# A graph network on one core: layer 1's softmax per eight graphs, reloaded one-hots, and the sum over edges as one pass over high and low halves

## The reference

```python
g_l = (h @ W_l.T).reshape(b, n, H, F)          # H = 8 heads, F = 16
g_r = (h @ W_r.T).reshape(b, n, H, F)
g_sum = g_r[:, :, None, :, :] + g_l[:, None, :, :, :]
e = jnp.einsum('bijhf,f->bijh', jax.nn.leaky_relu(g_sum, SLOPE), w_attn)
mask = adj_mat[..., None]
e = e * mask
e = jnp.where(mask == 0, -jnp.inf, e)
a = jax.nn.softmax(e, axis=2)
attn_res = jnp.einsum('bijh,bjhf->bihf', a, g_r)
out = jax.nn.leaky_relu(attn_res.reshape(b, n, H * F), SLOPE)
```

## Time and profile before

| | |
|---|---|
| median of 3 runs | 1712.24 us (1710.98 to 1717.81) |
| the profiled execution | 1710.04 us |
| its span, first to last instruction | 1708.3 us |
| busy: TensorE, its weight loads, VectorE, ScalarE | 1495.2, 1280.6, 1247.5, 977.0 us |
| mean granted TensorE clock, of full speed | 0.953 |

### The profile page before, as it was taken

The page is one execution under the profiler, slowest core; times in us unless marked ns, Lnnn a source line. Parts: engine busy times, 40 slices in busy tenths (PEclk is TensorE's granted clock), DMA queues, the critical chain, the costliest instruction groups (busy, mean ns, idle before and its releaser), DMA issues. The chain is left out here.

```text
span 1708.3 us, 32251 instructions
## 1 busy us (share of the span) xinstructions
PE 1495.2 (88%) x9961; PEld 1280.6 (75%) x9961; DVE 1247.5 (73%) x2330; ACT 977.0 (57%) x2551; POOL 4.9 (0%) x24
## 2 busy tenths in 40 slices
PE   3664889999999999999999985999999999998655
PEld 2553567778777787777788774999999999997554
DVE  4886667877878777878778853566666666666788
ACT  2564755665556565566656522666666666665554
POOL 0000000000000000000000000000000000000000
PEclk9897889999999999999999998999999999999787
DMA  3220534334433443343334303867667667671122
GB/s 81 63 62 14 213 144 182 153 144 158 175 143 143 161 173 143 143 186 148 143 150 178 145 32 131 314 238 255 247 239 255 243 244 252 241 256 38 56 74 68
DMA packets 100673, 274.61 MB, mean 161 GB/s; under 512 B 8800, under 2 KB 51424, under 8 KB 100576
## 3 DMA queue, kind: packets, MB, share of 16 engines
q1 hardware_dynamic: 100176, 273.52, 43.8%
q10 hardware_dynamic: 400, 0.00, 0.0%
HBM read 143.46 MB, written 130.02 MB: 160 GB/s over the span
## 5 line engine op out<-in xcount | busy, mean ns | idle before, releaser
L827 DVE TENSOR_TENSOR b_vv<-bank,b_vv 128x512 f32<-128x512 f32 (+1 forms) x192 | 113.7, 599 | 156.5 <-ACT b_vv L753 153.1
L1130 DVE TENSOR_REDUCE c_var<-c_ysq 128x4 f32<-128x512 f32 (+1 forms) x192 | 114.0, 594 | 117.0 <-ACT c_ysq L1078 94.4
L722 PE MATMUL bank<-b_wt,b_SIT 128*128 128x136 f32 x1280 | 161.4, 281 | 29.6 <-DVE b_SJ L452 23.2
L657 PE MATMUL wide<-b_vv,put_w 128*128 128x512 f32 (+1 forms) x384 | 171.5, 528 | 11.3 <-DVE b_vv L827 9.4
L722 PEld LDWEIGHTS bank<-b_wt,b_SIT 128*128 128x128 f32 x1280 | 152.8, 190 | 36.9 <-DVE b_SJ L452 23.4
L1020 PE MATMUL wide<-W2c,c_h 128*128 128x128 f32 x1280 | 174.0, 275 | 0.0
L1020 PEld LDWEIGHTS wide<-W2c,c_h 128*128 128x128 f32 x1280 | 169.6, 193 | 4.3
L686 PE MATMUL bank<-b_grs,b_SJ 128*128 128x128 f32 x1280 | 163.9, 286 | 4.2 <-ACT b_os L802 4.2
L686 PEld LDWEIGHTS bank<-b_grs,b_SJ 128*128 128x128 f32 x1280 | 159.6, 201 | 9.3 <-issue 5.1
L1050 PEld LDWEIGHTS bank<-c_z,c_SIT 128*128 128x128 f32 x1280 | 154.4, 194 | 5.5 <-DVE c_z L1138 2.3
L1050 PE MATMUL bank<-c_z,c_SIT 128*128 128x128 f32 x1280 | 155.0, 277 | 2.1 <-DVE c_z L1138 2.1
(11 more groups left out here) (212 smaller groups left out, 3154.9 us busy)
## 6 DMA issues: line engine op xcount, KB each, us to landing
si_d<-b_SI SPq DMA_DIRECT2D x64, 640.0 KB, 3.0
sj_d<-b_SJ SPq DMA_DIRECT2D x64, 640.0 KB, 4.0
sit_d<-b_SIT SPq DMA_DIRECT2D x64, 640.0 KB, 4.9
c_SJ<-sj_d SPq DMA_DIRECT2D x64, 640.0 KB, 4.1
c_SI<-si_d SPq DMA_DIRECT2D x64, 640.0 KB, 5.2
c_SIT<-sit_d SPq DMA_DIRECT2D x64, 640.0 KB, 4.3
xin<-in_x_dram SPq DMA_DIRECT2D x16, 256.0 KB, 3.0
ain<-in_adj_dram SPq DMA_DIRECT2D x16, 256.0 KB, 3.3
```

The lines of the kernel that those rows point to most:

```text
L657: pe.matmul(out, e.put_w[:, pos % Q, :], vv[:, (pos + k) % 2, 0:width(k)], start=(pos % Q == 0), stop=False)
L722: d = pe.matmul(ring[0][:, 0:W], s.SIT[:, ms, j, :], wt[:, (pos - LAG) % 2, j, :], start=(j == 0), stop=(j == TILES - 1))
L827: v.tensor_tensor(vv[:, b, 0:w], bU[b][:, 0:w], vv[:, b, 0:w], ALU.max).then_inc(v_ok, 1)
L1130: v.tensor_reduce(var[:, k, 0:r], ysq[:, k, 0:width(k)].rearrange("p (j f) -> p j f", f=P), AX.X, ALU.add).then_inc(sum_ok, 1)
```

## The change

- Softmax goes by R = 8 graphs: `score` puts eight graphs into 64 + 64 rows, and the scans run on 64 rows instead of 32, in halves of 640 edges, at positions 0, 1 and 2 of eight. The exponentials' transposes are ten, in transpose mode, at position 3, into two banks.
- The lag of the gather back is 11 steps, and the sum comes one step later. SJ keeps 4 buffers and SIT 2 instead of 8. Both, and g_r, are read back from HBM (SJl, SITl, grl), issued by SyncE's queue thirteen graphs later.
- `wt` is split: ScalarE copies it to F32R (`wh`, its first 136 columns: the high halves), VectorE subtracts (`wl_ok`: the low halves in the next 136). The sum is one F32R pass of 272 columns per tile. ScalarE copies both halves of the result (`ol`, `os`), and the finish adds them.
- The first 16 steps are written out instead of 8 (`every_step` gets `first`, 2 here), and `put_w` and `put_m` are made for 8 graphs instead of 4 in the setup.

```diff
@@ -522,22 +475,69 @@
         def sem(name):
             return c.enter_context(nc.semaphore("b_" + name))
 
-        LAG = 6
+        LAG = 11
+        R = 8
         W = P + HEADS
...
@@ -608,22 +605,33 @@
...
+                                     s.SIT[:, b, :, :]).then_inc(sit_out[b], 16)
+                    m, b, r = n - 13, (pos - 13) % 2, 16 * (4 * K + (pos - 13) // 2 + 1)
+                    if inner or 0 <= m < B:
+                        if inner or m >= 2:
+                            sp.wait_ge(o_mm, n - 14)
+                        sp.wait_ge(sj_out[b], r)
+                        sp.wait_ge(gr_out[b], r)
+                        sp.wait_ge(sit_out[b], r)
+                        sp.dma_start(SJl[:, b, :], e.sj_v[:, m, :]).then_inc(sj_in[b], 16)
+                        sp.dma_start(grl[:, b, :], e.gr_v[:, m, :]).then_inc(gr_in[b], 16)
+                        sp.dma_start(SITl[:, b, :, :].bitcast(F32), e.sit_v[:, m, :].rearrange("p (j i) -> p j i", i=P)).then_inc(sit_in[b], 16)
+
+                every_step(sp, step, 13, 2)
                 for b in range(2):
...
@@ -633,18 +641,18 @@
 
             @block.tensor
             def _(pe):
-                def transpose_exponentials(half):
-
-                    for j in range(TILES // 2 * half, TILES // 2 * (half + 1)):
-                        o = pe.matmul(ring[2][:, H * j:H * j + H], top[:, P * j:P * j + P], e.ident[0:H, 0:H],
-                                      start=True, stop=True)
-                    return o
+                def transpose_exponentials(bank, half):
+                    for j in range(TILES // 2):
+                        a = P * (TILES // 2 * half + j)
+                        o = pe.transpose(bank[:, H * j:H * j + H], top[:, a:a + P], e.ident[0:H, 0:H])
+                    o.then_inc(at_mm, 1)
 
                 def step(K, pos, inner):
...
@@ -654,41 +662,53 @@
                     def score(k):
                         pe.wait_ge(v_ok, 3 * n + k + 1)
                         out = bE[:, chunk(k)]
-                        pe.matmul(out, e.put_w[:, pos % Q, :], vv[:, (pos + k) % 2, 0:width(k)], start=(pos % Q == 0), stop=False)
-                        pe.matmul(out, e.put_m[:, pos % Q, :], s.SI[:, pos % 4, chunk(k)], start=False,
-                                  stop=(pos % Q == Q - 1)).then_inc(e_mm, 1)
+                        pe.matmul(out, e.put_w[:, pos, :], vv[:, (pos + k) % 2, 0:width(k)], start=(pos == 0), stop=False)
+                        pe.matmul(out, e.put_m[:, pos, :], s.SI[:, pos % 4, chunk(k)], start=False,
+                                  stop=(pos == R - 1)).then_inc(e_mm, 1)
 
                     if A:
...
-                            pe.wait_ge(s.sit_ok, 3 * n + 2)
+                            pe.wait_ge(s.sit_ok, 3 * n + 3)
                         if inner or m > 0:
                             pe.wait_ge(w_ok, 3 * m)
-                        transpose_exponentials(0)
                     if A:
                         gather(1)
-                    if transposed(n, pos, inner):
-                        transpose_exponentials(1).then_inc(at_mm, 1)
-                    if inner or 0 <= n < B:
+                    if T:
+                        transpose_exponentials(ring[2], 0)
+                        transpose_exponentials(ring[0], 1)
+                    if O:
+                        pe.wait_ge(wl_ok, 3 * o + 3)
+                        pe.wait_ge(sit_in[ob], 16 * (4 * K + (pos - LAG - 1) // 2 + 1))
+                        if A:
+                            pe.wait_ge(s.sit_ok, 3 * n + 1)
+                        for j in range(TILES):
+                            d = pe.matmul(ring[1][:, 0:2 * W], SITl[:, ob, j, :], wh[:, ob, j, :],
+                                          start=(j == 0), stop=(j == TILES - 1))
+                        d.then_inc(o_mm, 1)
+                    if A:
                         pe.wait_ge(s.sit_ok, 3 * n + 3)
                     if S:
+                        pe.wait_ge(sj_in[mb], 16 * (4 * K + (pos - LAG) // 2 + 1))
+                        pe.wait_ge(gr_in[mb], 16 * (4 * K + (pos - LAG) // 2 + 1))
                         if inner or m > 0:
                             pe.wait_ge(w_ok, 3 * m)
-                            pe.wait_ge(os_ok, m)
                         for k in range(CHUNKS):
-                            if k == 2 and transposed(n, pos, inner):
-                                pe.wait_ge(at_ok, batches(K, pos))
+                            if k == 0 and T:
+                                pe.wait_ge(at_ok, 2 * K)
+                            if k == 1 and O:
+                                pe.wait_ge(os_ok, o + 1)
                             for j in tiles(k):
                                 d = pe.matmul(ring[k][:, P * (j - 4 * k):P * (j - 4 * k) + P],
-                                              s.SJ[:, ms, P * j:P * j + P].bitcast(F32), grs[:, ms, :], start=True, stop=True)
+                                              SJl[:, mb, P * j:P * j + P], grl[:, mb, :], start=True, stop=True)
                             d.then_inc(g_mm, 1)
...
@@ -713,26 +733,15 @@
                         pe.matmul(pair_bank(pos, 1)[:, 0:2 * P], s.xT[:, :], e.WlrT[:, :, :], start=True, stop=True).then_inc(s.p_mm, 1)
                     if A:
                         score(2)
-                    if S:
-                        pe.wait_ge(w_ok, 3 * m + 3)
-                        pe.wait_ge(wa_ok, m + 1)
-                        if N:
-                            pe.wait_ge(s.sj_ok, 3 * g + 1)
-                        for j in range(TILES):
-                            d = pe.matmul(ring[0][:, 0:W], s.SIT[:, ms, j, :], wt[:, (pos - LAG) % 2, j, :],
-                                          start=(j == 0), stop=(j == TILES - 1))
-                        d.then_inc(o_mm, 1)
                     if N:
                         pe.wait_ge(s.sib_ok, g + 1)
                         pe.wait_ge(s.sj_ok, 3 * g + 2)
                         transpose_rows(pe, e, s, ring[1], 0)
...
@@ -752,26 +761,39 @@
                             act.wait_ge(e_mm, 3 * n + k - 1)
...
+                            act.wait_ge(w_ok, 24 * K - 24)
+                            act.wait_ge(wa_ok, 8 * K - 8)
+                        act.copy(aT[:, TILES // 2 * half:TILES // 2 * (half + 1), :],
+                                 bank[:, 0:TILES // 2 * H].rearrange("p (j c) -> p j c", c=H)).then_inc(at_ok, 1)
+
                     if A:
                         slope(0)
-                    if transposed(n, pos, inner):
-                        act.wait_ge(at_mm, i)
...
-                        if inner or n > Q:
-                            act.wait_ge(z_ok, i - 1)
-                        act.copy(es[:, :], bE[0:2 * H, 0:ECAP]).then_inc(es_ok, 1)
+                        if inner or n > R:
+                            act.wait_ge(z_ok, K - 1)
+                        act.copy(es[:, :], bE[:, 0:ECAP]).then_inc(es_ok, 1)
+                    if O:
+                        act.wait_ge(o_mm, o + 1)
+                        if pos % Q == 0 and (inner or o >= 2 * Q):
+                            act.wait_ge(s.cen_ok, fours(K, pos))
+                        act.copy(ol[:, (pos // Q + 1) % 2, pos % Q, :], ring[1][:, W:2 * W])
+                        act.copy(os[:, (pos // Q + 1) % 2, pos % Q, :], ring[1][:, 0:W]).then_inc(os_ok, 1)
                     if S:
-                        q = (pos - LAG) % Q
-                        act.wait_ge(at_ok, softmaxes(K, pos))
+                        r = (pos - LAG) % R
+                        act.wait_ge(at_ok, 2 * eights(K, pos))
...
-                        act.wait_ge(o_mm, m + 1)
-                        if (pos - LAG) % Q == 0 and (inner or m >= 2 * Q):
-                            act.wait_ge(s.cen_ok, i - 2)
-                        act.copy(os[:, parity(pos), (pos - LAG) % Q, :], ring[0][:, 0:W]).then_inc(os_ok, 1)
+                        for k in range(CHUNKS):
+                            js = slice(tiles(k).start, tiles(k).stop)
+                            act.wait_ge(w_ok, 3 * m + k + 1)
+                            act.wait_ge(wa_ok, m + 1)
+                            if inner or m >= 2:
+                                act.wait_ge(o_mm, m - 1)
+                            act.copy(wh[:, mb, js, 0:W], wt[:, mb, js, :]).then_inc(wh_ok, 1)
                     if N:
-                        if inner or g >= 8:
-                            act.wait_ge(o_mm, g - 7)
-                            act.wait_ge(sit_out[(pos + 1) % 2], 16 * (4 * K + (pos + 1) // 2 - 3))
...
@@ -816,39 +840,47 @@
...
                         w, b = width(k), (pos + k) % 2
                         v.tensor_tensor(vv[:, b, 0:w], bU[b][:, 0:w], vv[:, b, 0:w], ALU.max).then_inc(v_ok, 1)
 
-                    z = Steps(v, seq_z, 3 * (i - 1))
-                    if softened(n, pos, inner):
-                        z.n = 3
+                    z = Steps(v, seq_z, 5 * (K - 1))
+
```

(60 more changed lines are left out.)

257 lines of the change are left out of this document (138 added, 119 removed).

## The result

| | before | after |
|---|---|---|
| median | 1711.61 us (1710.22 to 1717.81, 4 runs) | 1746.82 us (1744.98 to 1747.83, 4 runs) |
| span of the profiled execution | 1708.3 us | 1745.9 us |
| mean granted TensorE clock | 0.953 | 0.921 |
| busy: TensorE, weight loads, VectorE, ScalarE | 1495.2, 1280.6, 1247.5, 977.0 | 1436.9, 1209.4, 1303.8, 1051.5 |

The changed kernel is slower: ratio 1.0187, 95% interval 1.0164 to 1.0211. That is inside the forecast's range (1688 to 1755) and on the side it held likeliest, but 29 us above the 1718 that it named, and outside its own case's 1704 to 1732. TensorE has 58 us less work, as the change intends, and the kernel takes 38 us more.

A forecast was written before the change was run, and what follows sets the result against it. It took each step as bounded by the longer of TensorE and VectorE, VectorE in most positions. Last split 61 us earlier, drain +67 and setup +1.5 gave +7.5 us, so 1718; range 1688 to 1755.

The forecast's parts named there:

- the side it held likeliest: Whole kernel: slower, chance 0.48, against 0.27 for within 0.5% of 1712 us and 0.25 for faster.
- its own case: Whole kernel: the forecast's main account without the rivals, 1704 to 1732 us, chance 0.50.
- TensorE's sum: Plain step of layer 1: ten F32R matmuls of 272 columns take 1.2 us instead of 2.32, making the step 10.4.
- VectorE's list: Layer-1 loop: VectorE needs 8.7 us every step plus finishes, residuals and softmax parts; it sets positions 0, 1, 2, 4, 5.
- a sign of being wrong: Layer-1 loop: the forecast called itself wrong if steps 6 and 7 took over 11.5 us.
- in a plain step they end some 2 us after the split: Plain loop step: row copies queued behind waiting high copies end before TensorE's gather back needs them, costing nothing.
- 10.4 + 1.1 + 0.8: Position 3 of eight: TensorE's plain step, ten exponential transposes, and copying out both halves, 12.3 us.
- The clock in the loop: Layer-1 loop: 4 us of occasional low clock as before, plus 7 us after the pauses of positions 0 and 1.
- a rival of 0.15: Positions 0 and 1: pauses bring 1.2 GHz work, losing 4 to 5 us per eight, +30, 1750 us; chance 0.15.
- The drain: End of layer 1: 118 us plus 15 for half clock, 133 in place of 66, +67 us.
- The transfers: DMA traffic grows from 2.0 to 3.5 MB per graph, 8.5 us of a step of 10.8 or more, costed at nothing.
- the start: Layer 1's steps 0 to 10, up to the split of graph 11: forecast to end at 280.5 us.

The follow-up runs named there:

- three edits: Changed kernel with exponentials' transposes one place later, the drain's chain ahead of maxima and finishes, and TensorE kept busy in positions 0 and 1: 1687.51 us, ratio 0.983.
- the busy gaps alone: Changed kernel with 36 small unread bf16 matmuls filling TensorE's pause in positions 0 and 1 of every eight: 1732.48 us, ratio 1.009.
- the run with another order: Changed kernel with the drain's high copies and low subtractions directly behind the multiplication, ahead of finish, residual, squares and maxima: 1720.29 us, ratio 1.0041.

## Why the prediction was right and wrong

**TensorE's sum: right.** 1.2 us were taken by the F32R row of 512 columns; the changed kernel's sum takes 1.25 at full clock (952.54 to the next gather at 953.79).

**VectorE's list: right in its items, 1.3 us per eight short in the sum.** Low subtractions 1.70 (1.63 forecast), half scans 1.47 to 1.53. With the clock full and the wait of position 3 away, the splits are:

| position | 0 | 1 | 2 | 3 | 4 | 5 | 6 | 7 | sum |
|---|---|---|---|---|---|---|---|---|---|
| forecast | 14.2 | 14.7 | 11.6 | 12.3 | 11.2 | 12.2 | 10.8 | 10.8 | 97.8 |
| three edits | 14.9 | 14.5 | 11.6 | 12.3 | 11.7 | 11.7 | 11.6 | 10.8 | 99.1 |
| after, two of five eights | 14.9 | 15.9 | 14.0 | 14.9 | 11.7 | 11.7 | 11.6 | 10.8 | 105.5 |

Position 0 was 0.7 low: VectorE waits 0.31 us ahead of the split and 0.41 ahead of the low subtractions, for ScalarE. Position 6 was 0.8 low, and its 11.6 is over the 11.5 that the forecast had named for positions 6 and 7 as a sign of being wrong. There the squares, the high copies and the row copies stand behind one another in ScalarE's queue: VectorE's low subtractions wait 1.2 us for the high copies, and TensorE's sum, which in its code also waits for the row copies, stands 0.8 us for them. From graph 11 to the last split the list gave 630.8 us, and the run with all three edits took 641.7.

**"in a plain step they end some 2 us after the split, and TensorE comes to that gather more than 3 us after it, so this costs nothing there": the first step that failed.** It is true of the plain step. The forecast priced position 3 as 10.4 + 1.1 + 0.8 and did not ask who else waits for the row copies: the transposes of exponentials do, in the same step that has the exponential in ScalarE's queue, and their wait stands ahead of a gather of pairs. It costs 2.6 us per eight, and the time fell by 15 us when the wait moved. The sum's wait in position 6, just named, is the same omission, 0.8 us per eight.

**The clock in the loop: the mechanism was right, its place half right, its size too small.** The forecast charged 4 + 7 us and made "+30" a rival of 0.15. Against the run with all three edits (641.7 us from graph 11 to the last split, nearly all at full clock) the changed kernel has 674.5; 13 of the 33 go with the row copies' wait alone, 13 with the busy gaps alone, and the last 7 only when both are gone. So the time of the rival, 1750, nearly came, and half by its own cause: half clock in positions 1 and 2 (1.4 and 2.4 us over the run at full clock in two of five eights, together 3.8 where the rival had 4 to 5; less in the others). The other half is the wait in position 3, which the rival didn't have and which itself lowers the clock. The Trainium skill, "TensorE: Matmul & The Clock Gate", section "Why this matters for your kernels", warned of idle gaps between bursts; the runs agree with its direction: the granted clock fell behind two waits of 1.82 and 1.76 us with 0.8 us of matmuls between. They also have waits of the same length behind which it stayed at 1.00, and what decides between the two isn't shown.

**The drain: right in its steps, and in its sum partly by luck.** 133 forecast, 137 measured, by the steps named: maxima, finishes and residuals ahead of the low halves (26 us, by the run with another order), the low halves' own chain, and the half clock. This last was put at 15, and 6 came back when most waits were filled. A plain step at full clock is 6.04 us (forecast about 6.0) in the run with all three edits, from its sums at 995.57 and 1001.61. The drain with most of its low clock away (130.6 us) is still some 12 us over the forecast's 118, so a clock term that was too large covered a chain that was too short; which of the special steps have the 12 us I haven't taken apart.

**The transfers: right.** The loop's waits have none for a reload, and 590 KB more per graph are hidden too.

In numbers: the last split came at 950 instead of 922. Of these 28 us, the start has -5 (the split of graph 11 at 275.6, forecast 280.5), the list +11 (641.7 for 630.8) and low clock with the wait of position 3 +22 (33 for the 4 + 7 that were charged). The drain has +4. The forecast counts the setup's 1.5 us apart, and the measured split contains them: 28 + 4 - 1.5 is the 30 us of span. The time lies in the range because the range took in the rivals; the forecast's own case, up to 1732, charged a third of what the low clock and that wait cost.

## What to carry to other kernels

When work moves from one engine to another, list for each moved or added instruction who waits for what stands behind it in its queue, in the special steps as well as in a plain one; here the argument for the plain step was right and the loop lost 2.6 us per eight in the one step with an exponential. A trade that pays in a full pipeline (VectorE's subtractions in a wait it had anyway) can cost where the pipeline drains, so choose the form of the work by stage: halves in the loop and F32 in the drain beat either alone. Look at the granted clock beside every pause that a change makes: behind waits of under 2 us, matmuls at half clock cost this loop up to 3.8 us per eight.
